# Attention on Trainium2: the softmax denominators copied by VectorE ahead of the output casts, and a fourth buffer for the probabilities

## What is computed

```python
c_kv = h @ W_dkv; c_q = h @ W_dq                      # 128 wide
k = concat(c_kv @ W_uk, rotary(h @ W_kr))             # 16 heads of 64
q = concat(c_q @ W_uq, rotary(c_q @ W_qr))
v = c_kv @ W_uv
scores = einsum('bqhd,bkhd->bhqk', q, k) / sqrt(64)
out = einsum('bhqk,bkhd->bqhd', softmax(scores), v) @ W_o + b_o
x = layernorm(h + out)
y = x @ quantize_int4(kernel) + bias + (x @ a) @ b
return layernorm(x + y)
```

## Time and profile before

| | us |
|---|---|
| median of the runs (3166.19 and 3166.96) | 3166.57 |
| profiled execution, its own time | 3174.5 |
| its span, core 3, the slowest | 3172.9 |
| spans of the eight cores | 3146.6 to 3172.9 |
| TensorE busy in matmuls | 2507.1 (79%) |
| ScalarE busy | 2195.4 (69%) |
| VectorE busy | 1150.4 (36%) |
| GpSimd busy | 233.4 (7%) |

### The profile page before, as it was taken

How to read it: one execution, slowest core, us unless ns; L and a number is a source line. 1 busy time by engine, 2 the same in 40 slices (tenths; PEclk the granted TensorE clock), 3 DMA queues, 4 the chain that set the end, 5 groups by cost and what they waited for, 6 DMA issues and landing times.

```text
span 3172.9 us, 40179 instructions; the slowest of 8 cores (3146.6 to 3172.9 us)
## 1 busy us (share of the span) xinstructions
PE 2507.1 (79%) x10584; PEld 788.9 (25%) x10584; DVE 1150.4 (36%) x1482; ACT 2195.4 (69%) x2481; POOL 233.4 (7%) x393
## 2 busy tenths in 40 slices
PE   3456659999888978898889888997888788988743
PEld 1222312222222222222222222222222222222211
DVE  1366222123343243324432434144323443344244
ACT  1233349999678967897679777986788687977600
POOL 4000000000000000000000000000000000010000
PEclk8566669999899989999999999998999899999956
DMA  6322230001212121212120122012121211121121
GB/s 107 113 98 83 77 75 26 19 20 52 70 39 69 36 86 37 72 35 64 56 76 25 49 73 77 30 45 82 45 61 42 70 54 58 35 78 55 55 91 40
DMA packets 89939, 188.44 MB, mean 59 GB/s; under 512 B 20579, under 2 KB 50532, under 8 KB 89476
## 3 DMA queue, kind: packets, MB, share of 16 engines
q1 hardware_dynamic: 44292, 82.81, 9.0%
q0 software_dynamic: 31616, 77.88, 8.5%
q10 hardware_dynamic: 13824, 25.17, 2.1%
HBM read 144.65 MB, written 51.64 MB: 62 GB/s over the span
## 4 chain that ended last, share of the span: by engine, by line
PE 53%; DVE 13%; ACT 11%; DMA 10%; issue 10%; POOL 1%; SPq 0%; DVEq 0%; ACTq 0%; POOLq 0%
PE PS L235 51%; ACT Psb L247 7%; DVE tA L252 3%; DVE bcast_sb L278 3%; PE PS L241 2%; ACT bcast_sb L247 2%; DMA bcast_sb<-rden 2%; DMA h<-h 1%; DVE h L252 1%; DMA rden<-bcast_sb 1%; DMA x_scr<-tA 1%; DMA rotq_scr<-c0s_sb 1%; DVE Qsb L258 1%; POOL Vsb L282 1%; DMA tA<-a_l 1%
## 5 line engine op out<-in xcount | busy, mean ns | idle before, releaser
L247 ACT ACTIVATE Psb<-PS 128x1024 bf16<-128x1024 f32 x2048 | 1980.6, 1043 | 473.0 <-PE PS L235 460.6
L235 PE MATMUL PS<-Psb,Vsb 128*65 128x512 bf16 x4096 | 1323.5, 406 | 114.5 <-ACT bcast_sb L247 98.3
L235 PE MATMUL PS<-Qsb,Ksb 64*128 64x512 bf16 x4096 | 828.3, 398 | 95.2 <-ACT Psb L247 87.7
L235 PEld LDWEIGHTS PS<-Qsb,Ksb 64*128 64x128 bf16 x4096 | 221.8, 93 | 955.5 <-issue 953.1
L235 PEld LDWEIGHTS PS<-Psb,Vsb 128*65 128x65 bf16 x4096 | 293.5, 112 | 611.4 <-issue 611.4
L278 DVE RECIPROCAL bcast_sb<-bcast_sb 128x512 f32<-128x512 f32 x64 | 214.4, 3351 | 270.0 <-DMA bcast_sb<-rden 269.9
L252 DVE TENSOR_TENSOR tA<-PS,h 128x512 f32<-128x512 f32 x128 | 88.4, 691 | 561.5 <-PE PS L235 522.8
L274 DVE CAST oun_sb<-PS 64x512 bf16<-64x512 f32 x128 | 87.3, 682 | 425.6 <-PE PS L235 423.5
L235 PE MATMUL PS<-wbuf,osb 128*128 128x512 bf16 x512 | 173.9, 428 | 71.5 <-DVE tA L252 54.9
L241 PE MATMUL PS<-ident_sb,h 128*128 128x128 f32 x512 | 106.5, 367 | 114.6 <-DMA h<-h 45.9
L228 POOL DMA_DIRECT2D rden<-bcast_sb x128 | 63.1, 498 | 1593.5 <-ACT bcast_sb L247 1571.8
(11 more groups left out here) (85 smaller groups left out, 1137.0 us busy)
## 6 DMA issues: line engine op xcount, KB each, us to landing
h<-h SPq DMA_DIRECT2D x64, 512.0 KB, 4.2
wbuf<-wo_p POOLq DMA_DIRECT2D x32, 512.0 KB, 6.0
bcast_sb<-rden POOLq DMA_DIRECT2D x128, 128.0 KB, 2.9
x_scr<-tA POOLq DMA_DIRECT2D x32, 512.0 KB, 3.0
wbuf<-wf_p POOLq DMA_DIRECT2D x32, 512.0 KB, 5.4
h<-x_scr SPq DMA_DIRECT2D x32, 512.0 KB, 3.8
out<-tA ACTq DMA_DIRECT2D x32, 512.0 KB, 2.7
o_dram<-oun_sb ACTq DMA_DIRECT2D x64, 128.0 KB, 1.7
```

The lines of the kernel that those rows point to most:

```text
L235: e.matmul(o, l, r, start=s1, stop=s2, tile_position=t, skip_group_check=k)),
L247: e.activation(o, i, f, scale=sc, bias=b)),
```

## The change

`ep_start` copies the denominators first and on VectorE (`cp` in place of `act`), and the casts of the output rows follow on the same engine. What waited for ScalarE's counter (`sAC`) for the denominators waits for VectorE's (`sDV`). The probabilities get four buffers in place of three: the three thirds of `Psb` and the first 1024 columns of `wkr_sb`; exp(G) then waits for PV(G-4).

```diff
--- before.py
+++ after.py
@@ -209,6 +209,8 @@
     qacc = x1T2[:, 1024:2048]
     qcmp = Psb[:, 0:1024]
     qsgn = Psb[:, 1024:2048]
+    PSB4 = [Psb[:, 0:1024], Psb[:, 1024:2048], Psb[:, 2048:3072],
+            wkr_sb[:, 0:1024]]
     qabs = wbufF[:, 1024:2048]
 
     S_ = Sched()
@@ -710,17 +712,16 @@
         def ep_start(PIDX2):
             lastG = PIDX2 * NKC + NKC - 1
             op_ = 512 * (PIDX2 % 2)
+            c1 = cp(bcast_sb[0:1, 0:512], PS[64:65, 2048:2560],
+                    waits=[("sPE", denb[lastG])] +
+                          ([("sDV", bcf_[PIDX2 - 1])] if PIDX2 > 0 else []))
+            c2 = cp(bcast_sb[32:33, 0:512], PS[64:65, 2560:3072])
+            dnev[PIDX2] = c2["sDV"]
             cp(oun_sb[0:64, op_:op_ + 512], PS[0:64, 2048:2560],
-               waits=[("sPE", denb[lastG])] +
-                     ([("qOD", norm_[PIDX2 - 2])] if PIDX2 > 1 else []))
+               waits=[("qOD", norm_[PIDX2 - 2])] if PIDX2 > 1 else [])
             e = cp(oun_sb[64:128, op_:op_ + 512], PS[0:64, 2560:3072])
             oune[PIDX2] = e["sDV"]
-            c1 = act(bcast_sb[0:1, 0:512], PS[64:65, 2048:2560], AF.Copy,
-                     waits=[("sPE", denb[lastG])] +
-                           ([("sDV", bcf_[PIDX2 - 1])] if PIDX2 > 0 else []))
-            c2 = act(bcast_sb[32:33, 0:512], PS[64:65, 2560:3072], AF.Copy)
-            dnev[PIDX2] = c2["sAC"]
-            return e["sDV"], c2["sAC"]
+            return e["sDV"], c2["sDV"]
 
         def ep_chain_gen(PIDX2, e_dv, c2_dv):
             op_ = 512 * (PIDX2 % 2)
@@ -731,7 +732,7 @@
             while gctr[0] < ph(2):
                 yield "spin"
             wdma0 = dma("gpsimd", rden[PIDX2:PIDX2 + 1, 0:512], bcast_sb[0:1, 0:512],
-                        sem="qBC", waits=[("sAC", c2_dv)] +
+                        sem="qBC", waits=[("sDV", c2_dv)] +
                         ([("qOD", norm_[PIDX2 - 1])] if PIDX2 > 0 else []))
             wdma = dma("gpsimd", rden[PIDX2:PIDX2 + 1, 512:1024],
                        bcast_sb[32:33, 0:512], sem="qBC")
@@ -779,30 +780,30 @@
         def emit_exp(p, kc):
             G = (qt * NP + p) * NKC + kc
             pi = G % 2
-            p3 = G % 3
+            p3 = G % 4
             w = [("sPE", sbd[G])]
-            if G >= 3:
-                w.append(("sPE", denb[G - 3]))
-            r = act(Psb[:, 1024 * p3:1024 * (p3 + 1)], PS[:, 1024 * pi:1024 * (pi + 1)],
+            if G >= 4:
+                w.append(("sPE", denb[G - 4]))
+            r = act(PSB4[p3], PS[:, 1024 * pi:1024 * (pi + 1)],
                     AF.Exp, waits=w, scale=0.125)
             expd[G] = r["sAC"]
 
         def emit_pv(p, kc):
             G = (qt * NP + p) * NKC + kc
             PIDX = qt * NP + p
-            p3 = G % 3
+            p3 = G % 4
             first = (kc == 0)
             lastk = (kc == NKC - 1)
             w = [("sAC", expd[G])]
             if first and PIDX > 0:
-                w += [("sDV", oune[PIDX - 1]), ("sAC", dnev[PIDX - 1])]
+                w += [("sDV", oune[PIDX - 1]), ("sDV", dnev[PIDX - 1])]
             mm(PS[0:65, 2048:2560],
                Vsb[:, 1040 * kc + 65 * (2 * p):1040 * kc + 65 * (2 * p) + 65],
-               Psb[:, 1024 * p3:1024 * p3 + 512], waits=w,
+               PSB4[p3][:, 0:512], waits=w,
                start=first, stop=lastk, tp=(0, 0))
             r = mm(PS[0:65, 2560:3072],
                    Vsb[:, 1040 * kc + 65 * (2 * p + 1):1040 * kc + 65 * (2 * p + 1) + 65],
-                   Psb[:, 1024 * p3 + 512:1024 * (p3 + 1)],
+                   PSB4[p3][:, 512:1024],
                    start=first, stop=lastk, tp=(0, 0))
             denb[G] = r["sPE"]
```

## The result

The changed kernel is slower: 1.0311 times the kernel before (95% interval 1.0294 to 1.0328), which is +98 us on 3166. The profiled execution took 3258.2 us with a span of 3256.6, 84 us more than the span before. It is the shortest execution of the changed kernel, and the one before, 3174.5 us, lay 8 us above its kernel's median, so the two spans differ by less than the medians do.

The account below looks back on a forecast made before the run. The prediction took TensorE as the bound (53% of the chain, ScalarE 11%), with waits at pair boundaries. Its terms, 64 - 19 + 35 = +80 us on a median of 3166.6, gave 3247 us, range 3205 to 3275 us.

Parts of the forecast that it names:

- The fourth buffer at nothing: P buffers: exp(G) waiting for PV(G-4) instead of PV(G-3) relaxes a wait that was never last; no cost or gain.
- Four copies in a row, +64 us: Pair boundaries: two denominator copies and two casts in series on VectorE, 0.71 us each, delay the first PV; +64 us.
- Round trip started early, -19 us: After boundaries: denominators start to DRAM and back 0.07 to 0.36 us sooner, so stalls behind the reciprocal shrink; -19 us.
- The clock, +35 us: TensorE behind boundaries: longer idle brings clock falls at about 53 of 56, 33 more than now; +35 us.
- Rival 5: TensorE behind boundaries: the deeper gap gives clock falls of twice the length, another 30 us, about 3280 us; chance 0.04.
- Rival 1: TensorE behind boundaries: no added falls of the clock, +45 us, 3212 us; chance 0.12.
- Rival 2: VectorE's denominator copies at boundaries: fast, 0.50 us each, +60 us, 3227 us; chance 0.07.
- Rival 3: VectorE at boundaries: copying one partition costs next to nothing, so not slower, -39 us, 3128 us; chance 0.01.
- Rival 4: ScalarE at boundaries: its 1.21 us of copies is truly gained, -68 us, 3099 us; chance 0.02.
- rival 6: Boundary waits: the change does nothing because the wait ends elsewhere; given no chance.

Follow-up runs that it names:

- the casts first: Changed kernel with VectorE's casts of the output rows ahead of the denominator copies; ratio 1.0301 to the kernel before.
- the filled wait: Changed kernel with six 512-column matmuls, result never read, ahead of the waiting first PV at each pair boundary; ratio 0.9996 to the kernel before.
- the kernel with the copies alone: Kernel before with only the denominator copies moved to VectorE ahead of the casts, three P buffers kept; ratio 1.0308 to the kernel before.
- the shorter wait: Changed kernel with denominator copies of 128 elements in place of 512 after the first pair; ratio 0.9996 to the kernel before.
- the single copy: Kernel before with both denominators in one ScalarE copy of 1x1024 and one transfer to DRAM; ratio 0.9849 to the kernel before.
- the piece of the tail: Kernel before with one piece of tail work placed between the kc = 2 scores and the waiting PV; ratio 0.9910 to the kernel before.

## Why the prediction came out right, and by which terms

The sum was +80 us; the two profiled spans differ by 84 and the eight cores' attention parts by 88.8. By the runs it is +98. The prediction put this at 3247 us and slower by over 2%, and that is how it came. That the sum lies within 9 us of the 88.8 is in part luck: the wait and the clock were put too low by 9 and 14 us, and what is given back was put too low by 14. Term by term:

- *The fourth buffer at nothing:* right, shown by itself (ratio 0.9992).
- *Four copies in a row, +64 us:* the mechanism is right, the size was +72.6. The copies took 0.71 us each as read from the cast. What was mis-sized is the release: I took 0.13 to 0.14 us, the way from ScalarE's end to PV, for VectorE too. It is 0.24 to 0.25, since the wait for the casts stands ahead of another one in TensorE's list, and that one costs 0.11 us although it is already met. So PV came 1.19 us later at an ordinary boundary, not 1.08; 1.45 to 1.55 later at most of the 14 where VectorE comes late, not 1.31; and 0.23 later where a query tile begins, where I had 0.
- *Round trip started early, -19 us:* the other idle times fell by 32.8 us, but not all where I had put it. The seven waits for `x1T` behind the reciprocal, 3.05 to 4.65 us before and 3.69 in the earlier trace rows, are all 3.05 now. With the seven for `tA` later in a pair they fell from 43.8 to 36.0 us, 7.8 us and not 19, and with the casts first they are back at 42.8, so this part is the early start. (The chain of the kernel before has 16 of these round trips, not 15 as I had counted.) Another 23.4 us are waits of over 1 us for exponentials, 60.6 us before and 37.2 now, which my sum did not have. With the casts first they stay low, 41.1 us, so most of them do not hang on the early start; whether they went because ScalarE is relieved of its copies or because TensorE comes later was not separated. The wait at the same place as in the earlier trace rows:

```profile
1305.68 1.40 DVE L276 CAST oun_sb<-PS 64x512 bf16<-64x512 f32 x2
...
1319.82 1.01 PE L237 MATMUL PS<-x1T,a_sb 128*16 128x128 bf16 x8 [3.05 <-DVE x1T L276]
```

- *The clock, +35 us:* +49. Here two errors lay against each other. I had concluded from 11 of 11 idle times between 2.1 and 3.2 us that falls would follow at 53 of 56 boundaries; in the trace it is 44 of 56 by the windows of 5 us. But 21 of these show 0.50 instead of 0.66: a longer fall, which I had only in a rival, and at a price of 30 us. Rival 5 came partly true. The 1.4 us of a short fall was read rightly from its two stretches; at 0.36 us for each us at half clock the 11.35 us at 0.85 would give 1.2 us.

Rival 1 (no added falls) is refuted by the filled wait and by the windows behind the boundaries. The Trainium skill (TensorE: Matmul & The Clock Gate, section HAM oscillation) looks at longer gaps. Here 2.94 us already costs. Rival 2 is refuted by the 685 ns. The Trainium skill (VectorE: DVE Perf Modes, section on why PSUM operands drop a tier) holds fp32 out of PSUM to the base rate. The trace agrees in kind: out of PSUM VectorE's casts of 128 and 512 elements take 278 and 682 ns, 1.05 ns for each element more, and out of SBUF those of 384 and 1024 elements 451 and 681 ns, 0.36 ns. Rival 3 falls by the same row. Rival 4 is refuted by ScalarE's idle time before the exponentials, 473.0 us before and 656.1 now in two groups (386.7 and 269.4), and rival 6 by the kernel with the copies alone.

## What to carry to other kernels

Take work off a busy engine only where the chain waits for it. Here two engines emptied the same columns of PSUM side by side and the later of the two set the wait; putting both jobs on one engine made the sum of them the wait, while the engine that was relieved then idled behind it.

An idle time of TensorE can cost more than its length. In this kernel 1.2 us more of waiting at 56 places came with 49 us of slower matmuls, and matmuls inside the wait, whose result nobody reads, gave 84 us back. Look at the granted clock behind each repeated wait, and put useful work there first.

## What the runs showed of the hardware

- Out of PSUM, VectorE's copy of 512 fp32 elements takes 685 ns on 1 partition and its cast 682 ns on 64; ScalarE's copy takes 591 ns, and 1.02 us for 1024 elements in one instruction against 1.21 for two of 512.
- A wait on a semaphore that is already met still costs TensorE's list 0.11 us when it stands behind the one that ends last: 2.94 us of idle time with two waits, 2.83 with one, and 2.83 with two of which the second ends last.
- In the 5 us behind the boundaries, where TensorE had idled for 1.75 us at most of them, the granted clock was down at 1.2 GHz for a time in 21.5 of 56 cases (mean of eight cores), and in 43 of 56 where it had idled for 2.94 us, there often for longer. With matmuls in these waits it was 0 and 7 of 56.
- One us at half clock cost 0.36 us in the change, 0.34 with the shorter wait, 0.35 with the filled wait and 0.41 with the single copy; with the piece of the tail, where only 39 us of half clock went, 0.53.
